# A router and two feed-forward layers on one Trainium2 core: the order in which three engines serve a 32-slot schedule

## The reference

```python
z = relu(x @ Wd + bd);  y = x + z @ Wu + bu
c = (y - mean(y)) * rsqrt(var(y) + 1e-5) * g + b
```

```python
probs = softmax(c @ gate_w + gate_b)
values, indices = top_k(probs, 2);  values /= sum(values) + 1e-9
out = x + c + mlp_shared(c) + sum over the two of value * mlp_expert(c)
```

## Time and profile before

| | |
|---|---|
| median of 3 runs | 626.38 us (625.54 to 627.92) |
| the profiled execution's own time | 622.08 us |
| its span, first to last instruction | 620.2 us |
| granted TensorE clock | 0.997 |
| PE busy | 594.8 us, 96% |
| DVE busy | 501.6 us, 81% |
| POOL busy | 413.3 us, 67% |
| ACT busy | 385.4 us, 62% |

### The profile page before, as it was taken

The page is one execution under the profiler, slowest core; times in us unless marked ns, Lnnn a source line. Parts: engine busy times, 40 slices in busy tenths (PEclk is TensorE's granted clock), DMA queues, the critical chain, the costliest instruction groups (busy, mean ns, idle before and its releaser), DMA issues.

```text
span 620.2 us, 16942 instructions
## 1 busy us (share of the span) xinstructions
PE 594.8 (96%) x5119; PEld 483.3 (78%) x5119; DVE 501.6 (81%) x1212; ACT 385.4 (62%) x660; POOL 413.3 (67%) x326
## 2 busy tenths in 40 slices
PE   7889979999999999999999999999999999999994
PEld 3556646667566678788888888888888899999883
DVE  4999848879977966898989898989897587887862
ACT  2686928758776845767676767676755455555541
POOL 4564587989885611477868686858697567666682
PEclk9999999999999999999999999999999999999998
DMA  8985656575244945667657656665644335343212
GB/s 285 322 220 150 159 161 183 161 235 115 78 138 153 328 114 171 144 113 149 116 127 133 147 127 127 132 136 128 94 53 72 60 61 66 58 67 64 44 21 32
DMA packets 116740, 81.31 MB, mean 131 GB/s; under 512 B 71090, under 2 KB 106162, under 8 KB 116658
## 3 DMA queue, kind: packets, MB, share of 16 engines
q1 hardware_dynamic: 100802, 60.64, 39.7%
q0 software_dynamic: 13296, 16.92, 15.2%
q10 hardware_dynamic: 2560, 2.69, 1.4%
HBM read 43.21 MB, written 24.42 MB: 109 GB/s over the span
## 4 chain that ended last, share of the span: by engine, by line
PE 68%; DVE 8%; POOL 8%; issue 8%; ACT 4%; DMA 2%; SPq 0%; POOLq 0%; ACTq 0%; DVEq 0%
PE Y L1527 30%; PE H L1501 29%; PE Y L1419 5%; POOL xs_rows L534 3%; PE H L1404 3%; POOL wreg L502 2%; POOL wreg L512 2%; DMA wreg<-in_vecs 1%; ACT hf L685 1%; DVE hl L1160 1%; POOL wreg L516 1%; ACT L685 1%; DVE wreg L808 1%; ACT wreg L623 1%; DVE wreg L949 1%
## 5 line engine op out<-in xcount | busy, mean ns | idle before, releaser
L755 ACT ACTIVATE hf<-H,prme 128x256 f32<-128x256 f32 (+1 forms) x312 | 149.2, 544 | 95.9 <-issue 80.5
L1501 PE MATMUL H<-xT,wreg 128*128 128x256 f16 (+1 forms) x1872 | 194.4, 263 | 0.2
L1527 PE MATMUL Y<-wreg,hh 128*128 x1136 | 188.3, 273 | 0.8 <-DVE hl L1255 0.8
L1501 PEld LDWEIGHTS H<-xT,wreg 128*128 x1872 | 169.0, 98 | 18.9 <-issue 1.0
L1527 PE MATMUL Y<-wreg,hl 128*128 x568 | 154.8, 273 | 0.0
L1527 PEld LDWEIGHTS Y<-wreg,hh 128*128 128x128 f16 x1136 | 111.1, 98 | 15.4 <-issue 1.5
L1255 DVE SCALAR_TENSOR_TENSOR hl<-hf,prme,hh 128x512 f16<-128x512 f32 (+1 forms) x156 | 115.8, 742 | 5.6
L1253 DVE TENSOR_SCALAR hh<-hf,prme 128x512 f16<-128x512 f32 (+1 forms) x156 | 91.1, 584 | 32.5 <-ACT hf L755 30.1
L588 POOL DMA_INDIRECT out_y<-hl,xgm x38 | 69.2, 1820 | 60.6 <-DVE hl L1282 40.9
L577 POOL TENSOR_SCALAR b2w<-b2t,wsel 128x256 f32<-128x256 f32 x71 | 97.9, 1602 | 15.1 <-DVE wsel L1270 9.6
L1404 PE MATMUL H<-xT,wreg 128*128 128x512 f16 x384 | 88.9, 379 | 6.8 <-ACT hf L685 4.7
(11 more groups left out here) (208 smaller groups left out, 663.6 us busy)
## 6 DMA issues: line engine op xcount, KB each, us to landing
stage<-in_w SPq DMA_DIRECT2D x16, 1024.0 KB, 6.2
b2t<-in_b SPq DMA_DIRECT2D x39, 128.0 KB, 3.3
wreg<-in_wpack SPq DMA_DIRECT2D x16, 256.5 KB, 4.7
wreg<-in_xt SPq DMA_DIRECT2D x16, 256.0 KB, 5.3
wreg<-in_vecs SPq DMA_DIRECT2D x16, 256.0 KB, 4.1
out_y<-wreg SPq DMA_DIRECT2D x16, 256.0 KB, 2.8
wreg<-in_x SPq DMA_DIRECT2D x14, 256.0 KB, 5.2
xs_rows<-wreg SPq DMA_DIRECT2D x9, 260.0 KB, 7.1
```

The lines of the kernel that those rows point to most:

```text
L755: act.activation(hf[:, c, half * w:(half + 1) * w], H[c][:, half * w:(half + 1) * w], ACT.Gelu_apprx_tanh, bias=pr[:, ch:ch + 1], scale=pr ...
L1501: m = pe.matmul(H[c][:, half * w:(half + 1) * w], we[:, bass.ds(e + h * 2048 + k * 1024 + col, P)], xp[:, a + k, 0:w], start=i == 0, stop= ...
L1527: m = pe.matmul(result(n, j), hx[:, n % 2, c * w + j * P:c * w + (j + 1) * P], we[:, bass.ds(e + 4096 + h * 2048 + c * D, D)], start=c == ...
```

## The change

Four things move; no instruction is added or taken away.

- Scatters of pair 0: blocks 1 to 3 went in slots 6, 7 and 7 ahead of `rows`; all four now stand in slot 5, block 0 ahead of `rows` as before and blocks 1 to 3 at the end of the slot. In the stream that is ahead of `root(3)` of slot 6.
- Scatters of pair 1 (slots 8, 9, 10, 10) move from behind `root` to the end of their slot, behind `rows`, `xb`, `residual` and `tokens`.
- On VectorE `weigh(p)` for all p above 0, and `choose(p)` for p from 2 to 6, go behind `low_h` of the same slot; `choose(7)` stays ahead of it. On ScalarE `exps(p)` for p from 2 to 6 goes one slot later, into the slot after `choose(p)`.
- On ScalarE `norm(1)` goes from the end of slot 0 to slot 1, behind its two `gelu` and ahead of its `high_h`.

```diff
 def block_slot(p, i):
 
+    if p == 0:
+        return 12
     if p < PT or p == NP - 3:
         return 12 + min(i, 2)
...
                 for p in at(s, 3):
                     root(p)
-                for p in range(PT):
-                    for i in range(4):
-                        if s == base(p) + block_slot(p, i):
-                            scatter(p, i)
+                if s == base(0) + block_slot(0, 0):
+                    scatter(0, 0)
...
-                for p in range(PT, NP):
+                for p in range(NP):
                     for i in range(4):
-                        if s == base(p) + block_slot(p, i):
+                        if p + i and s == base(p) + block_slot(p, i):
                             scatter(p, i)
...
                 gelu(t, 2 * q + 1)
+                if s == base(1) + 5:
+                    norm(1)
                 high_h(t, q)
...
+                for p in then(s, 9):
+                    if PT <= p < NP - 1:
+                        exps(p)
                 for p in then(s, 8):
-                    if p:
+                    if p in (1, NP - 1):
                         exps(p)
...
                 for p in at(s, 4):
-                    norm(p)
+                    if p >= PT:
+                        norm(p)
...
-                for p in then(s, 10):
-                    if p:
-                        weigh(p)
-                for p in then(s, 8):
-                    if p >= PT:
-                        choose(p)
+                if s == base(NP - 1) + 8:
+                    choose(NP - 1)
...
                 low_h(t, q)
+                for p in then(s, 10):
+                    if p:
+                        weigh(p)
+                for p in then(s, 8):
+                    if PT <= p < NP - 1:
+                        choose(p)
```

## The result

The changed kernel is slower: 633.14 us median of 4 runs (632.0 to 633.52) against 625.96 us (624.34 to 627.92), a ratio of 1.0104 with a 95% interval of 1.0062 to 1.0145. The forecast was 621.6 us. The profiled execution took 632.0 us with a span of 629.8, 9.6 us more than the 620.2 of before.

The account below looks back on a forecast made before the run. TensorE, busy 96% of the span, bounds the kernel; only its 7.1 us of waits from 45 to 235 us can be won. 4.0 + 1.34 + 0.64 = 6.0 gained, 1.2 lost: 626.4 - 4.8 = 621.6 us, range 619.0 to 625.8.

Parts of the forecast that it names:

- Part 2: `choose` and `weigh` behind `low_h`, `exps` a slot later: TensorE's waits of 1.34 and 0.64 us go.
- rival 3: Pairs 2 to 5: POOL's scatter waits for the later `weigh`, delaying `rows` through TensorE; 8.8 us lost, 630.4 us; chance 0.07.
- Behind `choose`: Nothing urgent stands there: `rank` comes a slot later on TensorE, behind a `gemm2` of 2.8 us.
- The wait of 1.34 us in slot 20: TensorE's `gemm2` waits for `low_h` of slot 19 behind `choose(5)`; it goes, bounds 1.34 gained or 0.
- that of slot 24 (0.64): TensorE's wait for `low_h` of slot 23; goes with `exps(6)` one slot later, bounds 0 and 0.64.
- Part 1, gain: Pair 0 and 1 scatters leave POOL's queue ahead of `rows`; `high_rows(3)` at 82.8, 3.50 and 0.52 us waits go: 4.0.
- Part 1, cost: Slot 8: `root(3)` 2.6 us late, transposes of pair 2 up to 1.3; 1.2 us for both, bounds nothing to 5.3.
- Part 3: `norm(1)` behind two gelu: 1.21 us wait at 37.07 goes, but 0 us won; bounds 1.2 gained, 1.4 lost.
- The sum: Whole kernel: 6.0 gained, 1.2 lost, 4.8 us; taken off the median 626.4 gives 621.6 us.
- rival 4: Pair 0's scatters held by VectorE: `root(3)` 14.4 late, 12.9 us of wait in slot 8, 633.3 us; chance 0.03.
- point from which it is wrong: Slot 8 costs over 3 us, ScalarE's waits for L512 in slots 12 to 20 grow, or TensorE waits before L1501.

Follow-up runs that it names:

- experiment 3: Kernel before with only `choose` of pairs 2 to 6 behind `low_h` and `exps` of those pairs one slot later, `weigh` unmoved: ratio 1.0123.
- experiment 7: Kernel before with only `choose` of pairs 2 to 6 moved behind `low_h`, `exps` unmoved: ratio 1.0121.
- experiment 11: The whole change with `choose` alone left ahead of `low_h`, against the kernel before: ratio 0.9985, 624.68 us against 625.63.
- experiment 2: Kernel before with `weigh`, `choose` and `exps` moved as in the change, scatters and `norm(1)` as before: ratio 1.0133.
- experiment 6: Kernel before with `choose` behind `low_h` and `exps` one slot later for pairs 2 to 4 only: ratio 1.0036.
- experiment 9: Experiment 3 with POOL's scatter block of slots 12, 19 and 22 put ahead of `rows`: ratio 1.0150 to the kernel before.
- experiment 12: The kernel before run once more, unchanged, for its profile: ratio 1.0024.
- experiment 8: Kernel before with only `exps` of pairs 2 to 6 one slot later: ratio 0.9987.
- experiment 5: As experiment 1, but block 3 of pair 0's scatters stays between `root(3)` and `residual`: ratio 0.9948 to the kernel before, 622.55 us against 625.2.
- experiment 4: Kernel before with only `weigh` moved behind `low_h`, for all pairs above 0: ratio 0.9989.
- experiment 1: Kernel before with only the scatters of pairs 0 and 1 moved as in the change: ratio 0.9962, 622.27 us against 624.4.

## Why the prediction was wrong

The step that failed is Part 2: "With `choose` behind, `low_h` can end 2.6 us earlier", and "Behind `choose` now stands nothing urgent". Moving `choose` was to gain 1.34 us and it costs about 1.2% (experiments 3 and 7), some 7.5 us; without it the change is not slower (experiment 11). Point by point:

- **`low_h` of slot 19.** It started where forecast, right behind `gain`, and ended at 161.0, where the earlier trace rows has 160.5; as slot 19 began 0.7 later, that is 0.2 us earlier in its slot and not 2.6. The prediction moved an instruction and kept its duration, though its rival 3 names a stretched `low_h`. `gain` releases POOL's `rows`, and the 2.58 us of `choose` were what VectorE did meanwhile at no loss. Shown: the durations (`low_h` of slot 22 took 3.7 us in the change and in experiments 2, 3 and 7, and 1.3 in before and in experiments 6 and 9, where no additions ran beside it for more than 0.2 us), that pairs 5 and 6 carry most of the loss, and, in slot 16 of experiment 9, that a stretch without a change of order costs TensorE time. Argued, by the account under experiment 6: that in slots 22 and 24 the stretch, not the order alone, is what the transposes pay for.
- **Behind `choose`.** Two things were urgent. `rank` needs its result: 1.32 us in slot 17, as `low_h` ahead of `choose` first waits for ScalarE, and the 2.8 us of `gemm2` that were to hide this did not suffice. And `low_rows` with its transposes stands behind both: they go out 3.2 and 6.7 us later than before, for 2.56 + 1.98 us of TensorE's waits (of the 6.7, 3.2 were there at `gain` of pair 7 already, 174.64 against 171.46). The prediction named the queue behind `choose` on TensorE and not that on VectorE, down to SyncE.
- **The wait of 1.34 us in slot 20** stayed, as 1.14, and was no fixed thing (0.35 in experiment 12); that of slot 24 (0.64) went, and one for `logits(7)` came in its place. `exps` alone is worth zero, within 0.3% (experiment 8).
- **Part 1, gain.** Right: `high_rows(3)` at 85.06 instead of 90.39 (forecast 82.8), slot 10 without a wait; 4.0 forecast, 4.4 measured in slots 9 and 10.
- **Part 1, cost.** The term of 1.2 us in slot 8 was mis-sized; slots 7 and 8 lost 3.5. The six scatters took 8.2 us (64.76 to 73.00; forecast 9.7) and `root(3)` came at 73.01 (forecast 73.8), so the queue was read well. What was missing is what stands behind `root(3)` once the scatters are gone: `residual`, beside which `roots(3)` takes 3.8 us instead of some 0.5 (experiment 5). In before the same `residual` met `gain` instead, 3.56 us, which became 1.28: the collision moved to where `low_h` stood right behind it. It is the same error as with `choose`. The transposes of pair 5 in the earlier trace rows had three scatters beside them, not four; nothing hangs on it.
- **Part 3.** The wait of 1.21 us went and slot 2 became no shorter, as forecast. It has no run of its own.
- **The clock.** The sum had no term for it. The profiled execution that it rests on, 4.3 us faster than the median, has no half-clock stretch in the first stage behind 45 us; the other one of the same kernel has two (experiment 12). A new hole therefore cost up to 1.7 us more than its length, and the removal of an old one brought as much more.
- **Rivals.** The two that ended near the measured time did so by other ways. Rival 3's wait stands in the trace of after (POOL idle 3.30 us before a scatter at 155.11) and is free as far as the runs tell: at 1.73 us in experiment 4, and at its full length in that experiments 2 and 3 differ by 0.1% only; for rival 4 the six scatters were too short. The "point from which it is wrong" that the prediction named first, slot 8 over 3 us, did come.

Experiments 1 and 5 are the fastest here, 0.4% and 0.5% under the kernel before.

## What to carry to other kernels

When an instruction is moved, don't carry its duration, or its neighbour's, to the new place: ask what the other engine runs there, and which operations tolerate it. A stretch of operations that don't collide, right behind the one that releases another engine's big operation, may be a cover; so may a DMA issue between a result and that engine's next big operation. Follow the queue behind a moved instruction to the last engine that it feeds (here VectorE, SyncE, TensorE), and compare several executions before a sum is made against one.

## What the runs showed of the hardware

- Operations of 0.15 us on 128x4 elements with two inputs from SBUF took 1.1 to 1.3 us each beside POOL's additions, as long as one of these; one with a single input kept its 0.18 us (experiment 5). A 128x1024 operation that starts 0.1 to 0.3 us ahead of two such additions takes 3.7 to 3.9 us instead of 1.28, and the additions keep their 2.48. It can go the other way: the pair at 166.65 in the change took 4.07 us, with `low_rows` begun at 166.11 and kept at 1.27, and `low_h` at 167.30, 2.29.
- TensorE's granted clock, between 45 and 235 us, fell to 0.50 for 3.41 us, once for 6.83 (experiment 4), around the end of a hole of 3.5 us (seven times), of one of 2.3 to 2.6, and once behind two of 1.1 and 0.9. The same hole of 3.50 us was followed by it in one execution and not in another.
